# First layer's attention: the causal limit by a table that VectorE adds with the row maximum and by selection on GpSimd, in place of mask products on TensorE

## What is computed

```python
def _reference_tuple_inner(x, W_dq, W_uq, W_dkv, W_uk, W_uv, W_o):   # 16 heads, head size 8
    k_eff = (W_dq.T @ W_uq.T @ W_uk).reshape(nh, hs, n_kvl)
    v_eff = jnp.transpose((W_uv.T @ W_o.T).reshape(n_kvl, nh, hs), (1, 0, 2))
    c_kv = x @ W_dkv.T
    q = (x @ W_dq.T @ W_uq.T).reshape(B, T, nh, hs)
    attn = einsum('bqhl,bkl->bhqk', q_lat, c_kv) / sqrt(hs)      # q_lat from q and k_eff
    attn = jnp.where(tril(ones((T, T))), attn, -jnp.inf)          # the causal limit
    attn = softmax(attn)
    y = einsum('bhqk,bkl->bhql', attn, c_kv)                      # then v_eff per head
x = x + attention(layernorm(x))
```

## Time and profile before

| | |
|---|---|
| three executions | 1378.89, 1382.06, 1384.43 us; median 1382.06 us |
| profiled execution | 1385.52 us, its span 1383.7 us |
| mean granted TensorE clock over the span | 0.854 of full |
| PE (matrix products) busy | 1087.8 us, 79% |
| DVE busy | 834.4 us, 60% |
| ACT busy | 567.7 us, 41% |
| POOL busy | 460.9 us, 33% |
| causal attention | from about 204 to 488 us of the span |
| twelve steps in the loop | 260.65 to 435.99 us |

### The profile page before, as it was taken

How to read it: one execution, slowest core, us unless ns; L and a number is a source line. 1 busy time by engine, 2 the same in 40 slices (tenths; PEclk the granted TensorE clock), 3 DMA queues, 4 the chain that set the end, 5 groups by cost and what they waited for, 6 DMA issues and landing times.

```text
span 1383.7 us, 16644 instructions
## 1 busy us (share of the span) xinstructions
PE 1087.8 (79%) x5478; PEld 705.5 (51%) x5478; DVE 834.4 (60%) x1706; ACT 567.7 (41%) x983; POOL 460.9 (33%) x378
## 2 busy tenths in 40 slices
PE   3999979999999959998677976407999677797630
PEld 2466765455555335666655755303455354675520
DVE  5667645566665356766685663336978938465422
ACT  2366632455554435665436653202111124564310
POOL 1255300000000004554436550164756404654035
PEclk9999986999998569999978997757989757998775
DMA  4022200000000201222104542210111111444212
GB/s 119 1 82 72 99 1 1 2 3 2 1 1 2 62 1 31 78 75 68 32 2 132 70 94 85 72 50 0 15 8 14 16 39 26 119 70 91 101 58 70
DMA packets 97721, 64.51 MB, mean 47 GB/s; under 512 B 39888, under 2 KB 82046, under 8 KB 97662
## 3 DMA queue, kind: packets, MB, share of 16 engines
q1 hardware_dynamic: 91774, 51.70, 12.5%
q0 software_dynamic: 5888, 12.07, 5.5%
HBM read 36.74 MB, written 12.06 MB: 35 GB/s over the span
## 4 chain that ended last, share of the span: by engine, by line
PE 52%; DVE 20%; issue 10%; ACT 8%; POOL 4%; DMA 3%; SPq 2%; another core or an unknown queue 1%; DVEq 0%; POOLq 0%
PE banks L1996 9%; PE banks L1865 5%; DVE normed L1151 5%; ACT hid_high L833 4%; PE banks L1563 4%; PE banks L1564 4%; PE banks L1565 4%; PE banks L1902 4%; POOL y_rows L725 4%; PE banks L1830 3%; PE banks L1854 2%; PE banks L1604 2%; DMA spare_dl<-d_low 2%; PE banks L1765 2%; PE banks L1680 2%
## 5 line engine op out<-in xcount | busy, mean ns | idle before, releaser
L1250 DVE TENSOR_TENSOR hid_low<-hid_full,hid_high 128x512 fp32r<-128x512 f32 x136 | 94.3, 694 | 136.5 <-ACT hid_high L875 119.5
L1363 DVE TENSOR_REDUCE mx<-banks 128x1 f32<-128x384 f32 (+3 forms) x256 | 117.8, 488 | 88.2 <-PE banks L1865 87.7
L713 POOL DMA_INDIRECT x_rows<-xn_d,idx_u x120 | 126.2, 1051 | 113.4 <-PE banks L1777 46.6
L933 ACT ACTIVATE wide<-banks 128x1024 f32<-128x1024 f32 (+3 forms) x128 | 90.0, 704 | 123.3 <-PE banks L1890 123.0
L1154 DVE TENSOR_TENSOR hid_low<-normed,hid_high 120x512 fp32r<-120x512 f32 x96 | 92.0, 958 | 67.0 <-ACT hid_high L833 67.0
L1996 PE MATMUL banks<-wide,consts 128*128 128x256 f32 x256 | 121.2, 642 | 7.4 <-issue 5.7
L725 POOL DMA_INDIRECT y_rows<-y_d,pos_u x64 | 60.9, 951 | 146.5 <-DMA y_d<-y_turned 127.6
L873 ACT ACTIVATE hid_full<-banks,be1c 128x512 f32<-128x512 f32 x96 | 66.8, 696 | 80.8 <-PE banks L1565 62.9
L833 ACT ACTIVATE hid_high<-normed 120x512 fp32r<-120x512 f32 x96 | 60.7, 632 | 87.4 <-DVE normed L1151 87.2
L1865 PE MATMUL banks<-aarena 32*128 32x384 f32 (+3 forms) x256 | 93.5, 405 | 0.0
L1996 PEld LDWEIGHTS banks<-wide,consts 128*128 128x128 f32 x256 | 58.2, 229 | 65.5 <-issue 55.5
(11 more groups left out here) (278 smaller groups left out, 2642.4 us busy)
## 6 DMA issues: line engine op xcount, KB each, us to landing
warena<-in_L_ffn_w_kernel SPq DMA_DIRECT2D x32, 344.0 KB, 3.3
y_d<-y_turned SPq DMA_DIRECT2D x30, 256.0 KB
warena<-in_L_ffn_wo_kernel SPq DMA_DIRECT2D x16, 300.0 KB
spare_uh<-u_high SPq DMA_DIRECT2D x14, 256.0 KB
spare_ul<-u_low SPq DMA_DIRECT2D x14, 256.0 KB
spare_dh<-d_high SPq DMA_DIRECT2D x14, 256.0 KB
spare_dl<-d_low SPq DMA_DIRECT2D x14, 256.0 KB
u<-in_L_ffn_We SPq DMA_DIRECT2D x1, 2048.0 KB
```

Of the source, the lines that this page charges most:

```text
L713: pool.indirect_dma_start(x_t[:, v % 3, k, :], None, xn_d[:, :], bass.IndirectOffsetOnAxis(ap=idx_u[:, 4 * v + k:4 * v + k + 1], axis=0))\
L1363: ins = dve.tensor_reduce(mx[:, j % 2, qt, r:r + 1], B[g % 2][:, at:at + P * (qt + 1)], AX, ALU.max)
```

## The change

The mask products go. For the row maximum, DVE adds a table instead: `CAUSAL` is 384 columns of zeros followed by the 128x128 mask, so its last n columns are the causal table of a block of n columns. One `tensor_tensor_reduce` adds table and scores, writes the sum back to the bank and gives the maximum. For the exponentials, POOL's `affine_select` sets what lies above the diagonal to zero in the four diagonal 128x128 blocks of `pt`, after ACT has written them and before `weigh` reads them; `weigh` waits for the new semaphore `sel` in place of `exp`. The loops on DVE and POOL are written out (12 steps one after the other); on PE and ACT they stay loops. The constants loaded at the start grow by 256 columns, and two conversions of masks go.

```diff
-CONST_PARTS = [("ident", P), ("upper", P), ("mask_qk", P), ("mask_kq", P), ("rev", E),
+CONST_PARTS = [("ident", P), ("upper", P), ("zeros", SEQ - P), ("mask_qk", P), ("rev", E),
...
+        CAUSAL = K[:, CONST_AT["zeros"][0]:CONST_AT["mask_qk"][1]]
...
+                zero = pool.to_reg(0.0)
+                def select(u, kt):
+                    pool.wait_ge(s["exp"], 8 * u + 2 * kt + 2)
+                    diagonal = pt[:, kt, :, P * kt:P * kt + P]
+                    pool.affine_select(diagonal, diagonal, [[0, 4], [1, P]], ALU.is_ge, zero, base=0, channel_multiplier=-1)\
+                        .then_inc(s["sel"], 1)
+                for kt in range(QT):
+                    select(0, kt)
+                for i in range(3):
                     for j in range(4):
-                        pool.wait_ge(s["pv"], 4 * i + j + 1)
-                        fill(i + 1, j)
+                        for kt in range(QT):
+                            select(4 * i + j + 1, kt)
+                            if kt == 1:
+                                pool.wait_ge(s["pv"], 4 * i + j + 1)
+                                fill(i + 1, j)
+                for u in range(13, UNITS):
+                    for kt in range(QT):
+                        select(u, kt)
...
-                dve.tensor_copy(mask_qk_b[:, :], const_part("mask_qk"))
-                dve.tensor_copy(mask_kq_b[:, :], const_part("mask_kq")).then_inc(consts_up, 1)
...
-                        ins = dve.tensor_reduce(mx[:, j % 2, qt, r:r + 1], B[g % 2][:, at:at + P * (qt + 1)], AX, ALU.max)
-                        at += P * (qt + 1)
+                        n = P * (qt + 1)
+                        part = B[g % 2][:, at:at + n]
+                        ins = dve.tensor_tensor_reduce(part, part, CAUSAL[:, SEQ - n:SEQ], 1.0, NEG, ALU.add, ALU.max,
+                                                       mx[:, j % 2, qt, r:r + 1])
+                        at += n
...
-                    for n, _ in enumerate(blocks):
-                        pe.matmul(bank[:, at + P * n:at + P * n + P], ident_b[:, :], mask_qk_b[:, :],
-                                  start=(n == 0), stop=False, skip_group_check=True)
...
-                    for k in range(2):
-                        pe.matmul(pairs[1 + rp][:, k, q0:q0 + P], ident_b[:, :], mask_kq_b[:, :],
-                                  start=True, stop=False, skip_group_check=True)
-
                     if beside is not None:
-                        rows_scores(*beside)
+                        rows(*beside)
...
-                    pe.wait_ge(s["exp"], 8 * u + 2 * kt + 2)
+                    pe.wait_ge(s["sel"], QT * u + kt + 1)
```

More of the change, by code:

```diff
@@ L133, in constants @@
     part("mask_qk")[:] = np.where(col > row, NEG, 0.0)
-    part("mask_kq")[:] = np.where(row > col, NEG, 0.0)
     part("cols")[:] = np.arange(P)
@@ L209, in program @@
         ones_b = sb("ones_b", [P, P], BF16)
-        mask_qk_b = sb("mask_qk_b", [P, P], BF16)
-        mask_kq_b = sb("mask_kq_b", [P, P], BF16)
         ones = sb("ones", [1, P])
@@ L398, in program @@
               "sh xg0 xg1 xg2 xt xh xl ys turned taken y_out0 y_out1 sw0 sw1 sw2 yg0 yg1 yg2 yg3 got x")
-        AT = ("v_ps v va a_full a_hi a_free mx_ps mx nm_hi nm nm_dma st exp pv os heads")
+        AT = ("v_ps v va a_full a_hi a_free mx_ps mx nm_hi nm nm_dma st exp sel pv os heads")
         MX = "qkv_ps qkv prod made sc_ps sub ex pv_free pv o o_out rows ot_ps ot out_ps x"
@@ L1033, in tables @@
                 dve.tensor_copy(ident_b[:, :], IDENT)
-                dve.tensor_copy(upper_b[:, :], const_part("upper"))
-                dve.tensor_copy(mask_qk_b[:, :], const_part("mask_qk"))
-                dve.tensor_copy(mask_kq_b[:, :], const_part("mask_kq")).then_inc(consts_up, 1)
+                dve.tensor_copy(upper_b[:, :], const_part("upper")).then_inc(consts_up, 1)
             parts = 0
@@ L1414, in attention @@
                 step(0, 0, 0, 7, "abm")
-                with dve.Fori(0, 3) as i:
-                    ch.loop(i, 4)
+                for i in range(3):
                     for n in range(4):
                         step(4 * i + 1 + n, i + (1 + n) // 4, (1 + n) % 4, 10 + 16 * i + 4 * n, "abmo")
-                    ch.end(3)
                 done = TILES - QT
@@ L1865, in rows_scores @@
                         ins = pe.matmul(bank[:, at:at + hi_k], qs[j][h, P * qt:P * qt + P],
-                                        ks[j][h, 0:hi_k], start=False, stop=True, skip_group_check=True)
+                                        ks[j][h, 0:hi_k], start=True, stop=True, skip_group_check=True)
                         at += hi_k
@@ L1870, in rows @@
                 def rows(u, j, g):
-                    rows_mask(u, g)
+                    pe.wait_ge(s["mx"], NMAX * u + g)
                     rows_scores(j, g)
@@ L1890, in scores @@
                         ins = pe.matmul(pairs[1 + rp][:, k, q0:SEQ], ks[j][h, P * kt:P * kt + P], qs[j][h, q0:SEQ],
-                                        start=False, stop=True, skip_group_check=True)
+                                        start=True, stop=True, skip_group_check=True)
                     ins.then_inc(s["st"], 1)
@@ L1913, in step @@
                     for x in range(8):
-                        if "b" in do:
-                            rows_mask(u + 2, MAX_FIRST[x])
-                        scores(u, j, x, ((j + 2) % 4, MAX_FIRST[x]) if "b" in do else None)
+                        scores(u, j, x, (u + 2, (j + 2) % 4, MAX_FIRST[x]) if "b" in do else None)
                         if x == 0 and "a" in do:
```

1 line of the change is left out of this document (removed).

## The result

The changed kernel took 1395.28 us, median of four runs (1390.67 to 1416.99), beside 1380.47 us for the kernel before on the same chip (1377.69 to 1384.43): ratio 1.0094, 95% interval 1.0051 to 1.0137. It is slower, by about 1%. The profiled execution took 1394.23 us, 8.7 us more than that of before.

What follows compares the result with a forecast made beforehand. PE was taken as the only full engine. Steps 0 to 12 -15.7 us, 13 to 15 with the last select -7.5, before step 0 +1.5, constants and loops +0.5: -21.2, 1364.3 profiled, so 1361 us predicted; range 1341 to 1400.

Steps and rivals of the forecast that it cites:

- the forecast case: Whole kernel: loop step 13.4 us and 1361 us, bounds 1354 to 1367; chance 0.42.
- the side that had a chance of 0.25: Whole kernel: slower, above 1389 us.
- The clock term: Loop: a few clock falls that the projections lift again, three of 7 us in 13 steps, 9 us, 0.7 a step.
- What goes: PE's loop step: without its 32 mask products it falls from 14.61 to 11.9 us (up to 12.9).
- What DVE gets: DVE's loop step: sixteen reductions become pairs, 0.1 us for main and 1.9 for small instructions, 9.85 to 11.9 us.
- rival 2: Loop: DVE becomes the bound, 15.1 us a step with twice the clock falls, 1385 us; chance 0.20.
- Hand-overs: Loop, PE and DVE through two banks: waits add 0.8 us a step (0.3 to 1.6), making it 12.7 us.
- What POOL gets: POOL: four selects a step of 0.9 us each (0.52 to 1.3), hidden by row scores and turned maxima.
- Steps 13 to 15: End of the attention: -4.5 us in step 13, -4 in 14 and 15, +1.0 for the last select: -7.5 us.
- Rival 3: Loop: clock lost as full-array mask products go, 21.2 us a step at 1.2 GHz, 1370 to 1462 us; chance 0.23.

Runs made afterwards that it cites:

- e16: The kernel before, all masks kept, with eight unused maxima over 128x512 added on DVE in each step: median 1492.77 us, ratio 1.096.
- e14: The changed kernel with two overwritten filler products of 128x32 weights ahead of each pair of scores: ratio 0.9803.
- e17: The kernel without any causal limit or fillers, each row maximum taken over only 128 columns of its block, lightening DVE: ratio 0.9615.
- e13: The changed kernel with four overwritten filler products reading only 32 partitions ahead of each pair of scores: ratio 0.9936.
- e9: The changed kernel with wide overwritten filler products (128x512) in steps 0 and 13 to 15 only: ratio 1.0028.
- e7: The changed kernel with one pair of overwritten 128x128 filler products ahead of every second pair of scores, 8 products a step: ratio 0.9966.
- e11: The kernel before, masks kept, with wide overwritten filler products in steps 13 to 15 alone: ratio 0.9967.
- e6: POOL selection only, row-score masks and plain maximum as before, wide fillers in steps 13 to 15: executions 1347.23, 1349.51, 1398.08 and 1398.67 us.
- e10: The changed kernel with eight 128x128 fillers at the first and fifth pairs of scores, and wide fillers in steps 0 and 13 to 15: ratio 0.9828.
- e8: The changed kernel with eight 128x128 fillers at the first and fifth pairs of scores of each step: executions 1331.75, 1332.73, 1374.39 and 1374.9 us.
- e15: The changed kernel with two 128x128 fillers ahead of each pair of scores and four unused maxima a step added on DVE: ratio 1.0389.
- e12: The changed kernel run again unedited: executions 1416.90, 1394.02, 1391.44 and 1350.37 us, median 1392.73, ratio 1.0096.

## Why the prediction was wrong

Forecast 1361 us, measured 1395.28: outside the forecast case, inside the range, and on the side that had a chance of 0.25. The profiled execution came 1394.23 - 1364.3 = 29.9 us above the forecast for it. The clock term alone was 42.8 - 12 x 0.7 = 34.4 us short over twelve steps.

- **What goes.** PE's own work a step was taken as 11.9 us; it is 11.90. Right.
- **What DVE gets.** Main instruction "like the reduction": 700 ns against 692, right. Small one 0.12 us: 0.140. But it begins before its main instruction ends and the next main one begins beside it, so hardly any of the 1.9 us priced for sixteen appeared: DVE's step came to 10.67 us, not 11.9. DVE did not become the bound (rival 2 falls). One price was missed: the addition of heads (L1398), two SBUF inputs, rose from 281 to 691 ns beside POOL's new work, 0.4 us a step. The Trainium skill's rule on shared ports, which the prediction cited and then used only in rival 2, covers this line, and the trace agrees.
- **Hand-overs.** 0.8 us a step forecast. PE idles 1.06 us. The step at 1.00 is 12.97 against 12.7: right in size, by luck in part. The forecast put the wait at the two banks; they account for 0.25 us, and the rest stands ahead of the key projection and the turned heads, behind other items of DVE's list.
- **What POOL gets.** 0.9 us a select, hidden: 0.64, and hidden.
- **Steps 13 to 15.** -7.5 us: from step 12 to the end it is 56.9 against 487.4 - 421.4 = 66.0 before, -9.1, of which 1.6 is step 12's own. Right.
- **The clock: the step that failed.** "I expect a few falls that the projections lift again", 0.7 us a step: three falls of 7 us. No row gave that number or that length. Measured: 42.8 us over twelve steps, 3.6 a step. The three falls came, but lasted 82, 14 and 22 us; the longest ran through three whole steps with two projections in each. Rival 3's price was near: for half of the time at the lower level it gave 1393 us, and the mean clock of 0.70 is 60% of the time; its step of 21.2 us measured 20.20.
- **Why it failed.** I priced the hand-over waits at their length. Where I judged the clock I named them ("gains waits") but gave them no weight of their own. e16 shows what they do: with about 1 us of waits a step the clock fell, masks or no masks, and each step at the lower level took 9.6 us more (25.25 against 15.69). In rival 3 I named the wrong mechanism, the loss of full-array work; e14, e16 and e17 refute it, and so does the profiled execution of e13. The mask products had held the clock by filling the time in which PE now waits for DVE.
- **The rule that I misread.** From a fall with PE busy 4.00 of 4.00 us I concluded that idleness does not matter and that by the page this term would be nothing. The row shows only that idleness is not the sole way to fall. The Trainium skill ("TensorE: Matmul & The Clock Gate", section on depth-cycling through PSUM banks) says that short idles between groups of products that cycle through banks make the clock come and go. That is e9's picture (12.97, 17.06 and 17.77 us in turn); in e16 the clock went and mostly stayed away. It spoke against this change, and my own 0.8 us of waits was its condition.

What stays open: step 13 of before falls with PE full; after a fall the clock stays low for anything from 10 to 154 us with PE full; and the same waits do not take the clock in every step. The change kept 1.00 for three steps from 336.92 with 1.06 us of waits in each, e7 for ten steps with 0.73, e13 through the loop with 0.7, while e16 lost it with 0.80. PE's busy share over a step does not by itself tell the clock. e11 has the plainest case of a wait: with the wide fillers PE was full at 1.00 to 453.7, then it waited 3.6 us for ACT and the clock fell.

```profile
449.70:453.70 4.00, 4.00 (x41) 1.81 (x39) 3.64 (x16) 1.67 (x2) 0.00 (x0) 1.00 0.00 0
453.70:457.40 3.70, 0.08 (x5) 0.05 (x2) 0.98 (x13) 2.62 (x4) 0.00 (x0) 0.81 0.00 0
457.40:461.40 4.00, 4.00 (x20) 1.95 (x24) 0.68 (x1) 2.70 (x4) 0.00 (x0) 0.50 0.00 0
```

Where the long executions of e6 and e13 lost it was not profiled.

## What to carry to other kernels

When you take work off the engine that bounds a loop, ask what that work was covering. If TensorE then waits about 1 us in 13 for another engine, price the waits at what they can do to the granted clock (here 43 us) and not only at their length. Look for the waits in PE's own rows: they need not stand where the work was taken out. Before giving such a change up, run it with cheap overwritten products in the waits: here they turned +0.9% into -1.7% (e10) and -2.0% (e14).

## What the runs showed of the hardware

- The lower level goes on after PE's waits have ended: stretches of 82 us (the change), 116 (e8) and 154 (e15) at 0.50 with PE full, or within 1 us of it. A stretch of 160 us in e15 and one of 306 in e16 began so and ran on into the end of the stage, where PE was not full.
- Executions of one program lie 3% and more apart, the longer ones at a lower mean clock: 1347 or 1398 us (e6), 1332 or 1374 (e8), 1350 or 1391 and more (e12).
- At half the clock PE's work takes 1.7 times as long: 20.20 / 11.90 = 1.70, and 25.25 / 14.61 = 1.73 in e16 against before.
- The add-and-maximum issues as two instructions, 700 and 140 ns at 512 columns, the second beginning 0.08 us before the first ends and the next addition at most 0.05 us after the second.
